# Accumulating DMAs for the sums of expert weights, and three layer norms moved from ScalarE to GpSimd, in a tiled attention and expert kernel

## The reference

```
x = x + cross_attention(layernorm(x), ctx)      # 16 heads, scores against 128 context rows of 96 features
x = x + tree_attention(layernorm(x))            # 16 heads, sigmoid paths of depth 5, causal softmax
x = x + experts(layernorm(x))
layernorm(x) = (x - mean) / sqrt(var + 1e-5)
# experts: q = x Wq + bq; for 8 heads: scores s1, s2 against 32 + 32 keys, top 10 of each,
# top 10 of the 100 sums, w = softmax over these 10;
# out = sum over heads and chosen experts of gelu(x . W_down[e]) * w * W_up[e]
```

## Time and profile before

| | us |
|---|---|
| runs | 1117.99 and 1122.17 |
| median | 1120.08 |
| profiled execution, its own time | 1122.6 |
| its span | 1119.4 |

### The profile page before, as it was taken

One profiled execution on the slowest core, in us unless ns is written; L12 is line 12 of the kernel. 1 busy time (PEld: TensorE's weight loads), 2 busy tenths in 40 slices (PEclk: granted clock), 3 DMA queues, 4 the chain that ended last, 5 costly groups with the idle time before them and its releaser, 6 DMA issues. The chain is left out here.

```text
span 1119.4 us, 36025 instructions
## 1 busy us (share of the span) xinstructions
PE 984.9 (88%) x12440; PEld 793.3 (71%) x12440; DVE 889.4 (79%) x2941; ACT 907.5 (81%) x2223; POOL 829.9 (74%) x871
## 2 busy tenths in 40 slices
...
GB/s 163 13 22 20 19 16 22 25 25 26 20 23 15 25 22 26 25 20 26 11 26 22 25 25 23 23 12 25 22 25 25 26 20 23 14 21 19 13 13 5
DMA packets 70369, 27.27 MB, mean 24 GB/s; under 512 B 47312, under 2 KB 69936, under 8 KB 70192
## 3 DMA queue, kind: packets, MB, share of 16 engines
...
q10 hardware_dynamic: 1040, 0.39, 0.1%
HBM read 14.47 MB, written 2.10 MB: 15 GB/s over the span
## 5 line engine op out<-in xcount | busy, mean ns | idle before, releaser
L1120 POOL TENSOR_TENSOR wsum<-wsum,mw 128x1024 f32<-128x1024 f32 x192 | 452.8, 2358 | 5.6
L1012 DVE SCALAR_TENSOR_TENSOR mw<-psF,cut,ew 128x1024 f32<-128x1024 f32 x256 | 326.4, 1276 | 49.8 <-ACT ew L795 49.7
L795 ACT ACTIVATE ew<-psF,lnz 128x1024 f32<-128x1024 f32 x256 | 283.6, 1120 | 15.0 <-PE psF L589 11.5
L589 PE MATMUL psF<-sel,usT 128*128 128x512 f16 x512 | 167.0, 411 | 33.0 <-DVE mw L1012 18.7
L1071 POOL TENSOR_TENSOR p<-p,rrow 128x512 f32<-128x512 f32 x128 | 133.1, 1040 | 74.5 <-DVE rrow L894 68.3
L705 ACT ACTIVATE p<-psXT,negmax 128x128 f32<-128x128 f32 x512 | 181.0, 377 | 3.2 <-DVE negmax L885 1.9
L377 PE MATMUL psXT<-cT,q 96*128 96x128 f32 x1024 | 144.5, 286 | 38.1 <-DMA cT<-cT_dram 31.8
L377 PEld LDWEIGHTS psXT<-cT,q 96*128 96x128 f32 x1024 | 132.7, 199 | 52.3 <-DVE q L626 41.8
L705 ACT ACTIVATION_READ_ACCUMULATOR p<-psXT,negmax 128x1 f32 x512 | 111.7, 218 | 0.0
L418 PE MATMUL psXT<-pT,c 128*32 128x384 f32 x768 | 98.7, 500 | 1.6 <-ACT pT L622 1.6
L885 DVE TENSOR_REDUCE negmax<-psXT 128x4 f32<-128x512 f32 x128 | 85.8, 670 | 16.4 <-PE psXT L377 16.4
...
## 6 DMA issues: line engine op xcount, KB each, us to landing
...
x<-x_dram SPq DMA_DIRECT2D x32, 64.0 KB, 2.2
xr<-x_dram SPq DMA_DIRECT2D x32, 64.0 KB, 1.9
y_dram<-y SPq DMA_DIRECT2D x32, 64.0 KB, 1.5
wqT<-wqT_dram SPq DMA_DIRECT2D x1, 512.0 KB, 5.0
wo<-wo_dram SPq DMA_DIRECT2D x1, 512.0 KB, 6.3
wdT<-wdT_dram SPq DMA_DIRECT2D x1, 512.0 KB, 3.6
```

The lines of the kernel that those rows point to most:

```text
L589: mm = pe.matmul(bank[BANK[f"e.s{h}"]][:, j * 512:j * 512 + 512], usT[:, t % 4, h, :], sel[:, j * 512:j * 512 + 512], start=True, stop=True)
L795: done(f"e.x{h}", act.activation(ew[:, h % NEW, :], bank[BANK[f"e.s{h}"]], ACT.Exp, bias=lnz[:, t % 4, h:h + 1]))
L1012: done(f"e.w{h}", dve.scalar_tensor_tensor(out=mw[:, h % NMW, :], in0=bank[BANK[f"e.s{h}"]], scalar=cut[:, t % 4, h:h + 1], in1=ew[:, h % ...
L1120: done(f"e.a{h}", pool.tensor_tensor(wsum[:, t % 2, :], mw[:, 0, :] if h == 1 else wsum[:, t % 2, :], mw[:, h % NMW, :], ALU.add))
```

## The change

The additions `e.a1` to `e.a7` go. Three DMAs issued from POOL take their place, `e.sa`, `e.sb` and `e.sc`: each adds two neighbouring slots of `mw` (1 MB, 8 KB per partition) onto the two slots that hold heads 0 and 1. `e.sa` adds heads 2 and 3, `e.sb` heads 4 and 5, `e.sc` heads 6 and 7; each waits for its masks and for the DMA before it. `e.fin` (POOL) then adds the two slots into `wsum`. `mw` grows from 4 slots to 10, used in a ring (`slot`). The three layer norms become two POOL instructions each, with the same names `x.norm`, `t.norm` and `k.norm`: the power as before, and one instruction over 128x128 that subtracts the mean and multiplies. The steps `x.root`, `t.root` and `k.root` and the three ACT instructions go. All five tables, BANK, and the waits that stand for shared banks are new to match; the largest lag falls from 7 to 5.

```
-NEW, NMW = 4, 4
+NEW, NMW = 4, 10
+SUMS = ("e.sa", "e.sb", "e.sc")
...
+        def slot(t, h):
+            return (FH * t + h) % NMW
...
             def w_turn(t):
                 after(pe, "e.w3", t + 1)
                 at_ends(pe, "e.add", t - 1)
-                pe.wait_ge(s[f"e.a{FH - 1}"], t + 1)
+                pe.wait_ge(s["e.fin"], t + 1)
...
-            def norm(name, i, src, slots, dst, root, turn):
-                def step(t):
-                    act.wait_ge(s[root], t + 1)
-                    after(act, turn, t - 2)
-                    done(name, act.activation(dst[:, t % 2, :], src[:, t % slots, :], ACT.Identity,
-                                              scale=rstd[:, i, t % 2, 0:1], bias=rstd[:, i, t % 2, 1:2]))
-                return step
...
             def mask(h):
                 def step(t):
                     dve.wait_ge(s[f"e.x{h}"], t + 1)
-                    if h < NMW:
-                        after(dve, f"e.a{h + FH - NMW}", t - 1)
+                    if h < 2:
+                        after(dve, "e.sc", t - 2)
+                    elif h < 4:
+                        after(dve, "e.fin", t - 1)
                     else:
-                        dve.wait_ge(s[f"e.a{max(h - NMW, 1)}"], t + 1)
+                        after(dve, "e.sa" if h < 6 else "e.sb", t - 1)
...
+            def layer_norm(name, i, src, slots, dst, stats, turn):
                 def step(t):
                     pool.wait_ge(s[stats], t + 1)
-                    after(pool, norm, t - 2)
+                    after(pool, turn, t - 2)
...
                     l.link(pool.tensor_tensor(rstd[:, i, t % 2, 0:1], mv[:, i, t % 2, 1:2], halfneg[:], ALU.pow))
                     l.wait()
                     pool.nop(nofuse=True)
-                    done(name, pool.tensor_scalar(rstd[:, i, t % 2, 1:2], mv[:, i, t % 2, 0:1],
-                                                  rstd[:, i, t % 2, 0:1], -1.0, ALU.mult, ALU.mult))
+                    done(name, pool.tensor_scalar(dst[:, t % 2, :], src[:, t % slots, :], mv[:, i, t % 2, 0:1],
+                                                  rstd[:, i, t % 2, 0:1], ALU.subtract, ALU.mult))
...
+            def add_pairs(name, h, before):
+                def step(t):
+                    for i in range(h if before else 0, h + 2):
+                        pool.wait_ge(s[f"e.w{i}"], t + 1)
+                    if before:
+                        pool.wait_ge(s[before], 16 * (t + 1))
+                    pool.nop(nofuse=True)
+                    to, by = slot(t, 0), slot(t, h)
+                    pool.dma_start(mw[:, to:to + 2, :], mw[:, by:by + 2, :], accum_op=ALU.add).then_inc(s[name], 16)
+                return step
+            steps["e.sa"] = add_pairs("e.sa", 2, None)
+            steps["e.sb"] = add_pairs("e.sb", 4, "e.sa")
+            steps["e.sc"] = add_pairs("e.sc", 6, "e.sb")
+
+            def add_last(t):
+                pool.wait_ge(s["e.sc"], 16 * (t + 1))
+                after(pool, "e.wturn", t - 2)
+                done("e.fin", pool.tensor_tensor(wsum[:, t % 2, :], mw[:, slot(t, 0), :], mw[:, slot(t, 1), :], ALU.add))
+            steps["e.fin"] = add_last
```

The tables (before with -, after with +; the number is the lag):

```
 ACT_ORDER = {
-    "t.pexp": 4, "x.e2": 3, "k.lnz": 5, "e.x2": 5, "e.x1": 5, "x.e0": 3, "e.x0": 5, "t.fsb": 4, "e.x3": 5,
-    "x.e1": 3, "t.exp": 4, "e.x4": 5, "x.e3": 3, "x.t0": 3, "t.csb": 4, "e.x5": 5, "x.t2": 3, "x.t1": 3, "e.x6":
-    5, "k.norm": 4, "y.u2": 3, "k.high": 4, "y.u0": 3, "y.u1": 3, "x.t3": 3, "x.norm": 2, "e.x7": 5, "y.u3": 3,
-    "x.high": 2, "e.gelu": 4, "k.shift": 4, "x.w0": 2, "x.w1": 2, "t.norm": 3, "x.w2": 2, "t.sb": 3, "k.eb": 4,
-    "t.v": 3,
+    "e.x1": 4, "x.e0": 2, "e.x0": 4, "t.fsb": 3, "e.x3": 4, "x.e2": 2, "x.e1": 2, "t.exp": 3, "e.x4": 4, "x.e3":
+    2, "x.t0": 2, "e.x5": 4, "t.csb": 3, "x.t2": 2, "x.t1": 2, "x.t3": 2, "e.x6": 4, "y.u2": 2, "e.x7": 4,
+    "k.high": 3, "y.u0": 2, "y.u1": 2, "y.u3": 2, "x.high": 1, "k.shift": 3, "e.gelu": 3, "t.sb": 2, "x.w1": 1,
+    "x.w0": 1, "t.pexp": 2, "x.w2": 1, "t.v": 2, "k.eb": 3, "k.lnz": 3, "e.x2": 3,
 DVE_ORDER = {
-    "e.add": 7, "k.z": 5, "t.path": 4, "x.x0": 3, "x.w3": 3, "e.w2": 5, "x.r2": 3, "e.w1": 5, "x.x1": 3, "x.r0":
-    3, "e.w0": 5, "e.w3": 5, "x.x3": 3, "x.r1": 3, "e.gate": 6, "t.div": 4, "e.w4": 5, "x.r3": 3, "t.res": 4,
-    "e.w5": 5, "x.stats": 1, "k.low": 4, "e.w6": 5, "k.top": 4, "k.split": 4, "x.low": 2, "e.w7": 5, "y.res": 3,
-    "k.cand": 4, "x.x2": 2,
+    "e.w2": 4, "x.w3": 2, "e.w1": 4, "x.x2": 2, "e.w0": 4, "x.x1": 2, "e.w3": 4, "x.r2": 2, "x.r0": 2, "e.gate":
+    5, "x.x3": 2, "x.r1": 2, "e.w4": 4, "t.div": 3, "x.r3": 2, "x.stats": 1, "e.w5": 4, "t.res": 3, "e.w6": 4,
+    "k.low": 3, "e.w7": 4, "k.top": 3, "x.low": 1, "k.split": 3, "y.res": 2, "k.cand": 3, "e.add": 5, "k.z": 3,
+    "t.path": 2, "x.x0": 1,
 POOL_ORDER = {
-    "e.a7": 6, "t.feat": 4, "x.n2": 3, "x.n0": 3, "e.a1": 5, "x.n1": 3, "e.a2": 5, "x.n3": 3, "k.root": 4,
-    "e.a3": 5, "e.a4": 5, "e.a5": 5, "k.inner": 4, "e.a6": 5, "t.root": 3, "x.root": 1,
+    "t.feat": 3, "e.sa": 4, "x.n0": 2, "x.n2": 2, "x.n1": 2, "x.n3": 2, "e.sb": 4, "k.norm": 3, "x.norm": 1,
+    "e.sc": 4, "k.inner": 3, "t.norm": 2, "e.fin": 4,
 PE_ORDER = {
-    "e.s2": 5, "e.s1": 5, "x.q3": 3, "x.s1": 3, "e.s0": 5, "t.fturn": 4, "e.s3": 5, "x.s3": 3, "t.sim": 4,
...
+    "x.s2": 2, "e.s0": 4, "t.fturn": 3, "e.s3": 4, "x.s1": 2, "t.sim": 3, "e.s4": 4, "e.wturn": 5, "x.s3": 2,
+    "x.p0": 2, "t.mix": 3, "e.s5": 4, "e.s6": 4, "x.p2": 2, "t.cturn": 3, "x.p1": 2, "x.p3": 2, "t.out": 3,
+    "y.m2": 2, "e.s7": 4, "y.m0": 2, "y.m3": 2, "k.turn": 3, "y.m1": 2, "k.key": 3, "x.turn": 1, "y.out": 2,
+    "e.hid": 3, "x.q0": 1, "e.out": 5, "x.q1": 1, "t.turn": 2, "x.q2": 1, "t.pv": 2, "e.s2": 3, "x.s0": 1,
+    "e.s1": 3, "x.q3": 1,
 SP_ORDER = {
-    "st.y": 7, "ld.ct": 2, "ld.c": 2, "k.kturn": 4, "ld.x": 0, "ld.xr": 2,
+    "ld.x": 0, "ld.c": 1, "ld.ct": 1, "k.kturn": 3, "ld.xr": 1, "st.y": 5,
```

More of the change, by code:

```diff
@@ L156, in after @@
             if 0 <= t < NT:
-                eng.wait_ge(s[name], 16 * (t + 1) if name in SP_ORDER else t + 1)
+                eng.wait_ge(s[name], 16 * (t + 1) if name in SP_ORDER or name in SUMS else t + 1)
         def done(name, ins):
@@ L318, in x_turn @@
             def x_turn(t):
-                after(pe, "y.u1", t - 1)
-                at_ends(pe, "y.u1", t - 2)
-                at_ends(pe, "y.u1", t - 3)
-                at_ends(pe, "y.u1", t - 4)
-                at_ends(pe, "y.u1", t - 5)
-                at_ends(pe, "y.u1", t - 6)
+                after(pe, "y.u0", t - 1)
+                at_ends(pe, "t.div", t - 2)
+                at_ends(pe, "t.div", t - 3)
+                at_ends(pe, "t.div", t - 4)
+                at_ends(pe, "t.div", t - 5)
+                at_ends(pe, "t.div", t - 6)
+                at_ends(pe, "t.div", t - 7)
                 pe.wait_ge(s["x.norm"], t + 1)
@@ L468, in feat_turn @@
                 pe.wait_ge(s["t.path"], t + 1)
-                after(pe, "x.e2", t + 1)
-                at_ends(pe, "y.u3", t)
+                after(pe, "x.w3", t + 1)
+                at_ends(pe, "y.u0", t)
                 pe.wait_ge(s["t.feat"], t + 1)
@@ L799, in _ @@
                 steps[f"e.x{h}"] = exp_sums(h)
-            steps["x.norm"](0)
             for j in range(4):
@@ L804, in _ @@
                                ACT.Copy, scale=QKSCALE).then_inc(own["setup_sb"], 1)
-            run(steps, ACT_ORDER, begun=(("x.norm", 0),), once={ACT_VO: setup_vo, ACT_KEYS: setup_keys})
+            run(steps, ACT_ORDER, once={ACT_VO: setup_vo, ACT_KEYS: setup_keys})
         @block.vector
@@ L865, in x_stats @@
                 dve.wait_ge(s["ld.x"], 16 * (t + 1))
-                after(dve, "x.root", t - 2)
+                after(dve, "x.norm", t - 2)
                 stat_chain["x.stats"].begin(t)
@@ L902, in add_cross @@
                 after(dve, "t.norm", t - 2)
-                after(dve, "t.root", t - 2)
                 l = stat_chain["y.res"]
@@ L1048, in _ @@
             steps = {}
[L1049 removed]
+            norm_chain = {n: Chain(pool, sem("pool_" + n.replace(".", "_")), 1) for n in ("x.norm", "t.norm", "k.norm")}
             li, lf = (Chain(pool, own[n], k) for n, k in (("pool_inner", 1), ("pool_feat", DEPTH)))
[L1052 removed]
+            def layer_norm(name, i, src, slots, dst, stats, turn):
                 def step(t):
                     pool.wait_ge(s[stats], t + 1)
[L1055 to L1056 removed]
+                    after(pool, turn, t - 2)
+                    l = norm_chain[name]
                     l.begin(t)
```

73 lines of the change are left out of this document (26 added, 47 removed), and 12 rows, old and new, of tables (BANK, PE_ORDER).

## The result

The kernel with the change takes 1285.86 us (median of 1281.99 and 1289.72) against 1120.08: ratio 1.148, 95% interval 1.141 to 1.156. The forecast was 1119 and its range ended at 1200. The profiled execution took 1281.99 us with a span of 1280.1, against 1119.4 before.

What follows compares the result with a forecast made beforehand. A ring of waits among in-order engines, not a full engine, bounds the kernel. Periods -5.6, fill -3 and tail +8.1 sum to -0.5 us: 1122.1 for a profiled execution, 1119 as median; range 1096 to 1200.

Steps and rivals of the forecast that it cites:

- Queues passed: Steps behind the new DMA issues: k.norm loses 0.2 us inside 0.3 of slack; k.kturn 3.2 us, e.s2 some 2 to spare.
- L: Time from when a 1 MB accumulating DMA may be issued to its landing: taken 7.3 us, bounds 5.2 and 9.7.
- the DMA ring: e.w2 to e.w5, e.sb, e.sc, e.fin, next e.w2: 16.9 + 2L, 31.5 us, hidden while L is below 7.5.
- The forecast for the tail: From the last tile's e.w5 to the end of its sums: 2L + 2.5 = 17.1 us against 9.0, 8.1 more.
- Rival 1: The DMA ring decides: at L = 9 e.w2 waits for e.fin each iteration, period 34.9, total 1204 us; chance 0.32.
- Rival 2: A DMA issue on POOL takes about 2.5 us, k.norm comes 1.2 us late, period 33.5, total 1157; chance 0.09.
- The walk of the ACT and key ring: One period: 18.5 us from e.x2 to k.high, 13.4 through the key chain to the next e.x2; 31.9 against 32.08.
- the dips of the clock: Lower granted TensorE clock in some periods, adding 0.39 us on average to an undisturbed period of 32.1.
- ACT's saving: ACT loses three norm instructions of 0.51 us, about 0.4 each with overlap: 1.2 us of its 27.9 a period.
- The norm's instruction: POOL's new 128x128 instruction for each norm: 0.3 us taken, so one norm lasts 1.0 us instead of 1.5.
- the fill: Start of the kernel: 1.5 us by norms, 0.5 by earlier k.shift, 1 from k.cand to masks, 3 us less.

Runs made afterwards that it cites:

- e1: Changed kernel with the DMA e.sc cut to 64 of its 1024 columns, part of the sums left out: 1175.3 us, ratio 1.049.
- e2: Changed kernel with the DMA e.sa cut to 64 of its 1024 columns, part of the sums left out: 1287.1 us, ratio 1.149.
- e13: e4 with the issue of e.sa put behind x.n0, x.n2 and x.n1 on POOL: 1134.1 us, ratio 1.011.
- e9: Changed kernel, DMAs whole, e.sc issued only after the next tile's k.kturn has landed, mw with 12 slots, e.fin adding in place: 1171.0 us, ratio 1.046.
- e14: e9 with e.sa issued behind x.n1 and the last tile's sums as additions on POOL: 1307.3 us, ratio 1.166.
- e4: Changed kernel with all three accumulating DMAs cut to 64 of 1024 columns, most sums left out: 1153.2 us, ratio 1.029.
- e6: e4 with the three norms back on ACT: 1183.0 us, ratio 1.056.
- e3: Changed kernel with the DMAs e.sa and e.sc cut to 64 of 1024 columns, e.sb whole: 1169.5 us, ratio 1.044.

## Why the prediction was wrong, point by point

**The failed step: "Queues passed".** It says that "`k.kturn` (3.2 us, rows 8) is now issued while `e.sc` moves; `e.s2` has some 2 us to spare behind it on PE". The spare was right: TensorE waits 3.2 us for a landing of 8.2, so it starts to wait at about 5.0, 1.8 beyond the old 3.2. The landing time was wrong: the sentence names the collision and then prices the transpose at its lonely duration. It took 5 us more. Those 5 less the 1.8 to spare are 3.2 us a period, and e1 measures 37.30 - 34.01 = 3.3: 102 us in 31 periods, 110.6 in the whole, with a tail that is 5 us shorter. The working bounded L, the DMA's own time, from both sides, and never its effect on another transfer, of which no row of before could tell. Its own figures give bounds as an estimate: with 4.1 us of moving in the way the transpose lands at 7.3, 2.1 past the 3.2 + 2 that it had to spare, 31 x 2.1 = 65 us; with the moving doubled at 11.4, 6.2 past, 192 us. The 102 us that were measured for this term lie between.

**L was right in the tail and 1.2 us short in the steady state.** In the tail, with nothing beside them, the issues of `e.sb` and `e.sc` and the start of `e.fin` of tile 31 are

```profile
1253.97 0.85 POOL L1117 DMA_DIRECT2D mw<-mw  x1 [6.73 <-DMA mw<-mw]
1261.55 0.85 POOL L1117 DMA_DIRECT2D mw<-mw  x1 [6.72 <-DMA mw<-mw]
1268.54 2.33 POOL L1126 TENSOR_TENSOR wsum<-mw 128x1024 f32<-128x1024 f32 x1 [6.14 <-DMA mw<-mw]
```

so one step is 7.58 and 6.99 us, taken 7.3. In the steady state it is 8.5 (617.54 to 626.00, 626.00 to 634.52), which is beyond the 7.5 up to which the prediction had the DMA ring hidden. The forecast for the tail was 8.1 more, it is 6.8 more. From issue to landing the rows have 7.7 us. The rule of the Trainium skill, Collectives: The Full Stack, "The bandwidth ceiling" (half the rate for a transfer with two source reads: an estimate of 6.8 us), comes nearer to it than the fit of the Trainium skill, DMA: Bandwidth & Descriptors, "Anatomy of one DMA" (an estimate of 4.4).

**Rival 1 had the direction, not the mechanism.** `e.w2` never waited for `e.fin` (above). At the steady L of 8.5 its formula gives 16.9 + 17.0 = 33.9 us, which the slower ring of 37.3 hid. By that formula the DMA ring too would have made the forecast period of 32.3 too short, by 1.6. No run isolated it; in e2 masks wait for `e.fin` 7 times, 11.2 us in all.

**Rival 2 was the wrong DMA.** An issue is 0.91 us of POOL by its own record. The power behind it starts 0.27 before that record ends and is 0.33 longer (0.88, not 0.55), so from 626.00 to 627.49 POOL has spent 0.94 more than the power alone takes; 1.2 was taken. But the price was charged to `e.sb` before `k.norm` only. `e.sa` stands before `x.n0` and waits for `e.w3`, and that was in no sum: 0.7 us a period, 22 us by the periods, 19 measured (e13), with issues that are 1.27 us long there and not 0.91. Nor was it said that `e.sb` waits for the landing of `e.sa`, with `k.norm` behind: in the kernel with the change shortening that wait gave nothing (e2), in e9 it is a link of the ring that is left, and in e14 it makes the ring.

**The walk of the ACT and key ring held but for one term.** It gave 31.9 us, 32.3 with the dips of the clock. With the moving away and `e.sa` out of the way of `x.n0` the mean period is 32.69 (e13), and one of its periods at a granted clock of 1.00 takes 32.70, 0.8 over. In that period `k.split` ends at 598.30 and `e.x2` starts at 605.61, 7.3 us as in the walk; but from there to `k.high` are 19.4 us, not 18.5, and ACT is idle in them, before `k.high`, for the turn of the late `k.norm`:

```profile
624.99 0.28 ACT L754 ACTIVATE xn3T<-psXT 128x128 f16<-128x128 f32 x1 [0.71 <-PE psXT L530]
```

In the kernel with the change ACT stands before `k.shift` for `k.split` 121.7 / 32 = 3.8 us, forecast about 4, and not before `k.eb` (1.5 us in all). ACT's saving was put at 1.2 a period; moving the norms measures 1.03 (e4 to e6).

**The norm's instruction was mis-sized**: 0.80 us where 0.3 was taken from a row over 128x80 with constants for operands; one norm is 1.5 us (0.56 + 0.17 + 0.80), not 1.0. So nothing is gained per norm in the fill, which came out 4.3 longer instead of 3 shorter. How much of that is the norm and how much the tables was not separated.

**The account of a period** (4.83 us more): `e.sc` moving beside `k.kturn` 3.3, `e.sa` moving 0.2, `e.sb` moving 0.4, `e.sa`'s issue ahead of `x.n0` 0.7, the rest of the tables 0.2. These are differences along one order of removal (after, e1, e3, e4, e13, before), each from one profiled execution; another order would share them out differently. They take in what the clock adds to each.
